# Two depth tiles of the first down projection, for the first half of the tokens, as plain fp32 matmuls instead of three matmuls of 12 bit parts

## What is computed

```python
gate = lora_add(einsum('bnh,fh->bnf', x, W_gate), x, A_gate, B_gate)
up   = lora_add(einsum('bnh,fh->bnf', x, W_up), x, A_up, B_up)
act  = silu(gate) * up
down = lora_add(einsum('bnf,hf->bnh', act, W_down), act, A_down, B_down)   # "first down projection"

nx = down * rsqrt(mean(down ** 2) + 1e-5) * ln_w
out = x + einsum('bsi,hi->bsh', silu(nx @ gate_w.T) * (nx @ up_w.T), down_w)
```

## Time and profile before

| | us |
|---|---|
| median of 3 runs | 397.53 (397.28 to 397.71) |
| profiled execution | 397.35 |
| its span, first to last instruction | 395.6 |
| TensorE busy in it | 392.0 (99%) |
| VectorE busy | 314.7 (80%) |
| ScalarE busy | 240.5 (61%) |

### The profile page before, as it was taken

How to read it: one execution, slowest core, us unless ns; L and a number is a source line. 1 busy time by engine, 2 the same in 40 slices (tenths; PEclk the granted TensorE clock), 3 DMA queues, 4 the chain that set the end, 5 groups by cost and what they waited for, 6 DMA issues and landing times.

```text
span 395.6 us, 5733 instructions
## 1 busy us (share of the span) xinstructions
PE 392.0 (99%) x1984; PEld 327.2 (83%) x1984; DVE 314.7 (80%) x476; ACT 240.5 (61%) x386; POOL 10.6 (3%) x13
## 2 busy tenths in 40 slices
PE   9999999999999999999999999999999999999997
PEld 5899888888888888888888888888888888888885
DVE  4799979586836769578699787878787869899994
ACT  4979786867574469815745656464646494484740
POOL 6300000000000000000000000000000000000000
PEclk9999999999999999999999999999999999999999
DMA  7540243311111551000400021313130216005112
GB/s 271 177 138 0 83 131 102 107 53 55 53 55 54 162 160 53 2 0 0 161 0 1 10 99 55 106 53 108 58 121 37 89 57 236 18 2 199 54 55 106
DMA packets 14942, 32.42 MB, mean 82 GB/s; under 512 B 2370, under 2 KB 4930, under 8 KB 14914
## 3 DMA queue, kind: packets, MB, share of 16 engines
q1 hardware_dynamic: 13792, 30.22, 23.6%
q10 hardware_dynamic: 1122, 1.84, 1.3%
HBM read 29.95 MB, written 2.10 MB: 81 GB/s over the span
## 4 chain that ended last, share of the span: by engine, by line
PE 99%; DVE 0%; issue 0%; DVEq 0%
PE bank L1363 53%; PE bank L1699 17%; PE bank L1589 14%; PE bank L1507 3%; PE bank L1553 3%; PE bank L1542 3%; PE bank L1373 3%; PE bank L1611 1%; PE bank L1603 1%; PE bank L1501 1%; PE bank L1618 0%; PE bank L1708 0%; DVE act L1354 0%; DVEq L1352 0%
## 5 line engine op out<-in xcount | busy, mean ns | idle before, releaser
L1363 PE MATMUL bank<-xs,ws 128*128 128x512 f32 x840 | 195.1, 390 | 0.0
L1363 PEld LDWEIGHTS bank<-xs,ws 128*128 128x128 f32 x840 | 156.5, 188 | 32.0 <-issue 0.2
L415 ACT ACTIVATE xs<-act 128x512 fp32r<-128x512 f32 x71 | 42.8, 624 | 21.1 <-DVE act L1045 7.5
L1589 PE MATMUL bank<-xs,wdc 128*128 128x512 f32 x240 | 55.7, 390 | 0.0
L1589 PEld LDWEIGHTS bank<-xs,wdc 128*128 128x128 f32 x240 | 44.8, 188 | 9.4 <-issue 0.2
L889 DVE TENSOR_TENSOR xs<-act,xs 128x512 fp32r<-128x512 f32 x71 | 47.6, 686 | 2.7 <-ACT xs L415 2.1
L889 DVE TENSOR_TENSOR ws<-wraw,ws 128x256 fp32r<-128x256 f32 (+2 forms) x45 | 30.0, 669 | 13.1 <-ACT ws L415 13.0
L415 ACT ACTIVATE mu<-bank 128x512 f32<-128x512 f32 x44 | 26.1, 596 | 20.2 <-PE bank L1363 13.7
L1699 PE MATMUL bank<-xs,vs 128*128 128x512 f32 x168 | 38.2, 389 | 0.0
L415 ACT ACTIVATE bank<-bank 128x512 f32<-128x512 f32 x30 | 17.3, 580 | 34.3 <-PE bank L1363 33.4
L1699 PEld LDWEIGHTS bank<-xs,vs 128*128 128x128 f32 x168 | 31.5, 188 | 6.5
(11 more groups left out here) (133 smaller groups left out, 439.6 us busy)
## 6 DMA issues: line engine op xcount, KB each, us to landing
wraw<-wgu_in SPq DMA_DIRECT2D x22, 512.0 KB, 3.3
wdr<-vs_in SPq DMA_DIRECT2D x7, 512.0 KB, 3.5
wraw<-vj_in SPq DMA_DIRECT2D x3, 896.0 KB, 4.5
wdr<-wd_in SPq DMA_DIRECT2D x10, 256.0 KB, 2.8
xa<-xT_in SPq DMA_DIRECT2D x4, 256.0 KB, 4.3
xa<-xT_in ACTq DMA_DIRECT2D x2, 512.0 KB, 4.8
bgu_raw<-bgu_in SPq DMA_DIRECT2D x32, 32.0 KB, 1.9
xres<-xT_in SPq DMA_DIRECT2D x4, 256.0 KB, 3.0
```

What stands on the lines that cost most here:

```text
L415: return nc.scalar.activation(out_ap, in_ap, ACT.Copy, scale=scale)
L1363: ins = mm(z[:, :], w_slot(j)[:, w, s, k * P:(k + 1) * P], xs[:, c, r, k, :], start=(start and k == 0 and s == 0 and r == 0), stop=(k == 1 ...
L1589: ins = mm(z[:, :], wd[:, s, h * P:(h + 1) * P], x[r], start=(start and s == 0 and r == 0), stop=False, skip_group_check=True)
```

## The change

For the first half of tokens, depth tiles n = 8 and n = 9 call `whole_c(n)` in place of `main_c(0, n)`. It makes one matmul for each of the four output tiles, with the fp32 weights as they arrived, `wdr[:, n % 2]`, and the fp32 activations, `act_at(ORDER_C[n], 0)`. The waits ahead of it and the semaphore behind it are the same. The splits of the two tiles' weights and activations are still made: `wdc[:, 8]` and `wdc[:, 9]` are also read for the second half of tokens.

```diff
+            def whole_c(n):
+                for h in range(4):
+                    ins = mm(Y_BANK[0][h][:, :], wdr[:, n % 2, h * P:(h + 1) * P], act_at(ORDER_C[n], 0),
+                             start=False, stop=False, skip_group_check=True)
+                return ins
+
             def t_c(t):
                 for n in range(FC):
                     for b in range(4):
@@ -1625,7 +1631,7 @@
             for n in range(10):
                 pe.wait_ge(s_alo, n + 1)
                 pe.wait_ge(s_wdlo, n + 1)
-                main_c(0, n).then_inc(s_use, 1)
+                (main_c(0, n) if n < 8 else whole_c(n)).then_inc(s_use, 1)
                 if n == 0:
                     p4(S1 - 1)
                 if n == 3:
```

## The result

The changed kernel takes 398.71 us (median of 9 runs, 398.24 to 399.16) beside 397.42 us (9 runs, 396.84 to 397.71) of the kernel before on the same chips: a ratio of 1.0034, 95% interval 1.0024 to 1.0044, or +1.3 us (+0.95 to +1.75). It is slower, as forecast, and lies at the lower edge of the range of 398.6 to 400.0. The profiled execution took 398.42 us, its span is 396.6 us.

What follows compares the result with a forecast made beforehand. TensorE's own instruction list was taken to bound the kernel: 7.09 us added less 5.46 us removed, switches at 0, gave +1.6 us, 398.95 us against the profiled execution or 399.1 against the median; range 398.6 to 400.0 us.

Steps and rivals of the forecast that it cites:

- The bound: Whole kernel: it ends when TensorE has worked off its list; around the change its matmuls wait for no other engine.
- Removed: Tiles 8 and 9: 24 matmuls of 512 columns in parts go, at 0.2274 us each, 5.46 us.
- Added: Tiles 8 and 9: eight plain fp32 matmuls, 16 instructions sending their columns through twice, 443 ns each, 7.09 us.
- my three: Three estimates of the net change in tiles 8 and 9: +1.50, +1.63 or +1.72 us; the middle one was taken.
- The ends of the price: Bounds for the eight new matmuls: one passage per instruction, -1.83 us; weight loads not covered, +4.44 us.
- Scaling the whole of L1603: Price from the low-rank part's plain fp32 line: 4 x 112 = 449 ns an instruction, 7.18 us for 16.
- rival (c): New matmuls' plain fp32 weight loads exposed: +4.4 us, 401.9 us; half exposed, some +3, 400.5 us; chance 5%.
- Switches: Changing into plain fp32 and out again around tiles 8 and 9: put at 0, with 0.55 us kept for the range.
- What else moves: ScalarE copies behind tile 9 slip 0.1 to 0.3 us, evictions 0.3 to 0.6 us; all of it costs nothing.
- (a): New matmuls faster: one passage per instruction, 16 x 0.227 = 3.63 us, -1.83 us, 395.7 us; chance 7%.
- (b): No change: low by low part left out of the new matmuls, three passages, 5.3 us, 397.4 us; chance 3%.
- (d): Absorbed in part: a wait taken for loose takes up to 0.6 us, so +1.0 us, 398.5 us; chance 3%.

Runs made afterwards that it cites:

- +0.7: Kernel before with only tile 9 in plain fp32 and tile 8 still in parts; one run, 397.83 us beside a median of 397.38.
- +5.6: Kernel before with tiles 2 to 9 in plain fp32, weights read from their rounded high part; 403.36 us beside 397.38, ratio 1.0148.
- the run with -3.64 us: Kernel before with tiles 8 and 9 of the first half reduced to the high by high product; 394.43 us, ratio 0.9929.
- all ten tiles shortened: Kernel before with all ten tiles of the first half reduced to the high by high product; 395.44 us, ratio 0.9960.
- the new order: Ten tiles in high by high products only, weight loads of tiles 6 to 9 issued ahead of twelve small SyncE loads; 393.07 us, ratio 0.9880.

## Why the prediction was right, and where it was off

**The bound** held. No matmul waits in the changed kernel, and the span behind the change is 234.7 us in it, in the kernel before and in the runs with +0.7 and +5.6 us ahead of it alike (+5.6 for the eight tiles: +1.4 ahead of the low-rank part and +4.2 behind it).

**Removed**, 24 x 0.2274 = 5.46 us: exact. 72 matmuls became 48, and 16.59 - 11.15 = 5.44 us.

**Added** was the mis-sized term. The mechanism, two instructions with two passages each, fits every run above the floor, but the forecast's 7.09 us were 6.87, 429 ns an instruction and not the 435 to 450 foretold. (The trace gives 0.834 ns for a column; that this is two passages at full speed, and not one at half speed, is a reading, and the time is the same either way.) Two numbers taken from products of parts don't hold for the other kind: 0.421 ns a column where the plain kind has 0.417 (16 instructions, 0.06 us), and 12 ns fixed where it has 2.4 (0.15 us). I had the better number in hand: L1603's 4 ns. I set it aside because its weights have another shape, and it was the kind that counted, not the shape. The low end of my three, +1.50, was nearest to the measured +1.43.

**The ends of the price.** Scaling the whole of L1603 (+1.72) was too high since it multiplies by four also what doesn't grow with the columns: 112 ns less 107 ns for 2 x 128 columns is 5 ns, which became 20. The exposed weight load, rival (c), is refuted at this size. The floor of 111 ns an instruction is as near as the runs come to it; by the prices above I estimate that it is covered from some 130 columns in plain fp32 and some 235 in parts.

**Switches** cost nothing that counts (8 ns each), as taken. The stall around L1603 is that part's own.

**What else moves.** The two copies `hi_ac(18)` and `hi_ac(19)` and the evictions behind them in the changed kernel, beside rows 7:

```profile
158.40 1.35 ACT L415 ACTIVATE xs<-act 128x512 fp32r<-128x512 f32 x2
159.78 2.75 ACT L415 ACTIVATE nx<-bank 128x512 f32<-128x512 f32 x4
```

The pair takes 1.35 us instead of 1.16, so the second copy now waits 0.2 us for tile 9's count, as forecast. But ScalarE came to the pair 0.68 us earlier in this execution, of which 0.44 us are the earlier start, so the second copy ends no later than before (159.75 us beside 160.24): there was a wait and no slip. The four evictions are through at 162.5 us, at 162.3 before, in an execution that is 0.4 us earlier at this place: some 0.6 us later, as forecast. All of it is hidden.

**Rivals.** (a), faster, falls: an instruction of 512 columns follows the other after 429 ns, and the low-rank part obeys its columns. The rule of half rate for FP32_LOW_HIGH ("Perfetto Trace Analysis", Engine Utilization, in the Trainium skill), read for a whole matmul, falls with it; read for each of the two instructions it agrees. The price of (a), -1.83 us, would have come through whole, though VectorE and ScalarE are full there: the run with -3.64 us shows that the splits stand in the way only from about 2.7 us on. (b) falls by the 16 equal records, and by 6.87 us where it has 5.3. (d) falls by the 234.7 us.

The forecast of 399.1 was 0.4 us above the median: 0.2 us are the fixed part, 0.1 us the median of the kernel before (397.42 over nine runs, not 397.53 over three), and the rest is less than the measurement resolves.

## What to carry to other kernels

On a TensorE that never waits, price an edit by cadence read from the same kind of instruction, even of another shape. Here a plain fp32 matmul of 512 columns costs 0.86 us and three products of parts 0.68 us, so the plain kind would pay only where it takes splits away that something waits for; this change kept the splits. And before pricing a saving rather than a cost, ask where the next engine stands: here 2.7 us ahead, so 3.6 us less work gave about 2.9. 18.2 us less gave only 1.9: the splits let 3.6 us through, and the lower clock behind the long waits took some 1.5 us of that back.

## What the runs showed of the hardware

- Float32r and plain fp32 matmuls that each come with a 128 x 128 weight load start no closer than 111 ns from each other, in four runs: 64 and 128 columns in plain fp32, 128 columns in parts, 192 and 128 mixed. The load's record says 188 to 192 ns all the same.
- Products of parts carry 12 to 14 ns besides their columns at 512 and 256 columns (227.4 and 119.6 ns), plain fp32 2.4 ns. Why isn't settled; the runs show only that it isn't the floor of 111 ns.
- With the end of a wait of 2.9 us (all ten tiles shortened), and of one of 2.4 us (the same with the new order), TensorE's granted clock fell to 0.5. It was at the lower level for some 10 us and again for some 3 in the first run, for more than 12 us in the second, where 24 matmuls of 256 columns took 5.49 us and not 2.87. Waits of 0.67 and 1.00 us earlier in the first run, and the one of 0.69 us in the run with two tiles shortened, left the clock at the upper level.
